# Scores of two narrow cross attentions as two 64-row groups, with half the head columns in the keys

## The reference: what is computed

```
q = x @ w_q + b_q        (4, 256, 16, 8)
k = ctx @ w_k + b_k      (4,  64, 16, 8)
v = ctx @ w_v + b_v      (4,  64, 16, 8)
scores = q . k / sqrt(8) per head; in layer 0 masked positions are replaced
x = layernorm(x + softmax(scores) @ v @ w_o + b_o)
```

## Time and profile before

| what | value |
|---|---|
| median of 3 runs | 1954.29 us (1953.05 to 1954.43) |
| the profiled execution | 1955.33 us, of which the profile's span is 1953.6 us |
| PE busy | 1400.2 us (72% of the span) |
| DVE busy | 1194.9 us (61%) |
| ACT busy | 694.5 us (36%) |
| POOL busy | 440.2 us (23%) |
| granted PE clock, mean | 0.835 of 2.4 GHz |
| `l0x`: keys block starts, attention starts, attention ends | 531.3, 537.8, 583.6 us |
| `l1x`: keys block starts, attention starts, attention ends | 899.8, 906.2, 948.8 us |

### The profile page before, as it was taken

How to read it: one execution, slowest core, us unless ns; L and a number is a source line. 1 busy time by engine, 2 the same in 40 slices (tenths; PEclk the granted TensorE clock), 3 DMA queues, 4 the chain that set the end, 5 groups by cost and what they waited for, 6 DMA issues and landing times. The chain is left out here.

```text
span 1953.6 us, 23816 instructions
## 1 busy us (share of the span) xinstructions
PE 1400.2 (72%) x8378; PEld 1055.8 (54%) x8378; DVE 1194.9 (61%) x2335; ACT 694.5 (36%) x1421; POOL 440.2 (23%) x454
## 2 busy tenths in 40 slices
PE   5888888988686985836719847587268738863785
PEld 3666666666563654714509735465237516732572
DVE  5899999999255664155595464334458277437744
ACT  3465665565132761312302220042033233423341
POOL 2566556565102002101003110000010050005000
PEclk8999899999796996967859868599679867976697
DMA  6101110110101002500014200000100000000000
GB/s 208 34 26 39 40 34 26 40 34 1 56 1 33 1 1 82 163 2 1 13 43 160 83 0 1 1 1 32 55 0 1 1 0 1 1 1 0 1 1 11
DMA packets 31030, 59.85 MB, mean 31 GB/s; under 512 B 6592, under 2 KB 17856, under 8 KB 30656
## 3 DMA queue, kind: packets, MB, share of 16 engines
q1 hardware_dynamic: 29888, 56.09, 8.9%
q0 software_dynamic: 1024, 2.23, 0.5%
HBM read 54.13 MB, written 4.18 MB: 30 GB/s over the span
## 5 line engine op out<-in xcount | busy, mean ns | idle before, releaser
L187 POOL TENSOR_TENSOR rstd<-spread,minus_half 128x4 f32<-128x4 f32 x36 | 36.8, 1023 | 960.5 <-DVE spread L169 960.5
L917 PE MATMUL l0h_scores<-l0h_k_rot,l0h_q_slots 128*128 128x128 f32 (+1 forms) x1024 | 206.9, 349 | 0.0
L917 PEld LDWEIGHTS l0h_scores<-l0h_k_rot,l0h_q_slots 128*128 128x128 f32 x1024 | 169.8, 208 | 13.2
L1134 POOL TENSOR_TENSOR l0h_k_part<-large_weights,l0h_sines 128x512 f32<-128x512 f32 x64 | 83.9, 1311 | 177.1 <-PE l0h_scores L917 129.1
L1008 ACT ACTIVATE l0h_scores<-l0h_scores,l0h_top 128x128 f32<-128x128 f32 (+1 forms) x256 | 100.4, 392 | 27.7 <-DVE l0h_top L1087 27.5
L1081 DVE TENSOR_TENSOR l0h_q_slots<-l0h_q_rot,l0h_chosen 128x1024 f32<-128x1024 f32 x64 | 78.4, 1225 | 6.7
L893 PE MATMUL l0h_projected<-XT,l0h_wq 128*128 128x256 f32 x256 | 70.1, 397 | 15.2 <-ACT large_weights L979 11.9
L1135 POOL TENSOR_TENSOR l0h_k_rot<-large_weights,l0h_cosines 128x512 f32<-128x512 f32 x64 | 80.8, 1263 | 0.0
L907 PE MATMUL l0h_scores<-l0h_key_masks,l0h_query_picks 4*128 4x128 bf16 (+1 forms) x256 | 45.0, 257 | 49.0 <-DVE l0h_probs L1104 49.0
L1087 DVE TENSOR_REDUCE l0h_top<-l0h_scores 128x2 f32<-128x256 f32 (+1 forms) x128 | 65.0, 546 | 6.6 <-PE l0h_scores L917 6.4
L1446 ACT ACTIVATE l0n_probs<-l0n_scores,l0n_top 128x256 f32<-128x256 f32 x128 | 53.8, 482 | 39.0 <-DVE l0n_top L1477 38.9
(11 more groups left out here) (718 smaller groups left out, 3658.7 us busy)
## 6 DMA issues: line engine op xcount, KB each, us to landing
l1e_experts<-in_l_experts SPq DMA_DIRECT2D x16, 768.0 KB, 4.4
l0e_experts<-in_l_experts SPq DMA_DIRECT2D x15, 578.0 KB, 4.5
l0h_chosen<-l0h_chosen_dram SPq DMA_DIRECT2D x64, 128.0 KB, 3.0
small_weights<-in_w_l_ffn SPq DMA_DIRECT2D x1, 4016.0 KB, 12.9
l0h_pos<-l0h_pos_dram SPq DMA_DIRECT2D x56, 64.0 KB, 2.0
large_weights<-in_w_l_xattn SPq DMA_DIRECT2D x1, 2632.0 KB, 9.1
l0h_wq<-in_l_wq SPq DMA_DIRECT2D x16, 128.0 KB, 2.9
large_weights<-in_w_l_attn SPq DMA_DIRECT2D x2, 512.0 KB, 4.1
```

The costliest lines, as they stand in the source:

```text
L917: mm = nc.tensor.matmul(at[:, slot], q_slots[:, s % 2, slot, part, i * P:(i + 1) * P], k_rot[:, s % 2, part, 0:KEYS[i][1]], start=False, s ...
L1134: nc.gpsimd.tensor_tensor(k_part[:], source, at_batch(sines, s), ALU.mult)
```

## The change

`keys` gets eight head columns for each batch where it had sixteen. Column j keeps head j on partitions 0 to 63 and head j + 8 on partitions 64 to 127, and is zero elsewhere. The scores of heads 0 to 7 are then a product over partitions 0 to 63 alone, into the first bank, and those of heads 8 to 15 a product over partitions 64 to 127, into the second. In layer 0 both mask products now come first, then the two score products.

```diff
-        keys = sb("keys", [P, B, HX, SC])
+        keys = sb("keys", [P, B, HX // 2, SC])
...
-                    nc.vector.tensor_tensor(keys[:, b], bc(k_t[:, b * SC:(b + 1) * SC].unsqueeze(1), [P, HX, SC]),
-                                            bc(k.own_head.unsqueeze(2), [P, HX, SC]), ALU.mult)
+                    nc.vector.tensor_tensor(keys[:, b], bc(k_t[:, b * SC:(b + 1) * SC].unsqueeze(1), [P, HX // 2, SC]),
+                                            bc(k.own_of_eight.unsqueeze(2), [P, HX // 2, SC]), ALU.mult)
...
                     if mask:
                         nc.tensor.matmul(out[:, c, :], k.ident16[:], bc(mask(t).unsqueeze(1), [P, HX // 2, SC]),
                                          start=True, stop=False, skip_group_check=True)
-                    mm = nc.tensor.matmul(out[:, c, :], q_t[:, t * P:(t + 1) * P], keys[:, b, c * 8:(c + 1) * 8, :],
-                                          start=not mask, stop=True, skip_group_check=True)
+                for c in range(2):
+                    half = slice(c * P // 2, (c + 1) * P // 2)
+                    mm = nc.tensor.matmul(out[:, c, :], q_t[half, t * P:(t + 1) * P], keys[half, b], start=not mask, stop=True,
+                                          skip_group_check=True)
```

## The result

The changed kernel takes 1946.93 us (median of 14 runs, 1942.21 to 1951.14), the kernel before 1953.22 (14 runs, 1950.52 to 1957.53). The ratio is 0.9968, 95% interval 0.9958 to 0.9978: 6.3 us faster, between 4.3 and 8.2. The time lies in the range of the prediction (1937.5 to 1949), and the sign is the forecast one, but the gain is about half of the 11.8 us of the sum.

A forecast was written before the change was run, and what follows sets the result against it. The prediction took DVE plus some POOL to bound the keys block and PE the steady attention. Keys 4.3, steady 2.7 + 2.0 and start 1.3 + 1.5 sum to 11.8 us: median 1942.5 us, range 1937.5 to 1949.

The forecast's parts named there:

- if the clock is below 1.00 between the first turn and the last score: A sign, in the profile of the attention after the change, that would show the prediction wrong; no size given.
- What bounds the stretch: Steady attention: PE sets the pace; after the change still in `l0x`, while in `l1x` ACT's copy ends last.
- Keys: Keys blocks: shorter DVE instructions, done after 2.92 us, end each block 2.13 us earlier; 4.3 us for two.
- Overlap of the two halves with 512 columns: Attention scores: 64-row passes of the two halves run two at a time, 0.43 us from pair to pair.
- no overlap: Rival on the scores: the halves do not overlap with 512 columns; about 1955 us, no change; chance 0.07.
- Price of the ways in and out: Attention units: switching to 64-row passes and back costs 0.41 us a unit; units become 4.36 and 4.03 us.
- The start: Scores at half clock before the first turn: 1.3 us saved in `l0x` and 1.5 in `l1x`, together 2.8 us.
- the clock comes up later: Rival: the clock rises later against the first turn, or later stages meet it differently; 4 us, 1946.5 us; chance 0.10.
- the clock falls: Rival in the steady stretch: half clock as PE idles; both stretches falling entirely gives 1967 us or so; chance 0.03.

The follow-up runs named there:

- masks apart: The changed kernel with each bank's mask product again right ahead of its score product; ratio 1.0039 to the kernel before, 7.6 us slower.
- sixfold one: The changed kernel with projections, keys block and attention run six times in each part, each after some 10 us of DVE-only work; median 2597.83 us.
- the keys alone: The changed kernel with eight head columns kept, but scores as full-array products over all 128 rows; ratio 0.9983 to the kernel before.
- the extra products: Unneeded PE products ahead of the first turn, in the keys block, or both, added to the changed kernel: ratios 0.9946, 0.9939, 0.9930 to the kernel before.
- products in the keys block: The changed kernel with two products of 512 float32 columns on PE while it waits for the keys; ratio 0.9939 to the kernel before.
- groups only: The kernel before, keys still with sixteen columns, but scores as two 64-row groups; ratio 0.9993 to the kernel before.

## Why the prediction was right, and by how much it was off

The terms of the sum came out nearly as worked out in the profile, except that the clock took a part of the gain back at the first turns, and the measured gain is about half of the sum. The time still lies in the range because the range was wide, 5 to 17 us, and not because this loss was counted in it. By a sign that the prediction named itself ("if the clock is below 1.00 between the first turn and the last score") its part on the clock was wrong: the clock was at 0.50 in 545.0 to 548.4 and in 906.7 to 910.2.

- **What bounds the stretch**: right. PE sets the pace in `l0x`, and in `l1x` the bound went from PE to the chain of turn, copy and W.
- **Keys**: right to 0.01 us in the profile: 2.92 us, PE's start 2.13 us earlier. POOL's instructions still end one by one beside DVE's, with four left after it. Alone it brings 3.3 us measured, 4.3 forecast, inside the interval.
- **Overlap of the two halves with 512 columns**: right, 1.13 us for four passes, and masks apart shows that adjacency is what makes it. The rival "no overlap" is out. The pairs start 0.53 us apart (551.99 and 552.52) and not 0.43, but the block as a whole takes the 1.06 us that the sum had.
- **Price of the ways in and out**: right. The units are 4.35 and 4.03 us for 4.36 and 4.03 forecast. The Trainium skill ("TensorEngine Tiling (Array Packing)", Key Properties) states that a change of the tiling mode drains TensorE. The trace agrees as far as a unit pays some 0.4 us around its 64-row passes, the price of the rows, and that does not decide.
- **The start**: DVE's first reduce comes 3.06 and 2.12 us after PE's start, 3.1 and 2.3 forecast, and the first turn follows as worked out, 1.40 and 1.68 us earlier after PE's start than before. This is the term that failed all the same: "Both lie on the chain that leads to the first turn", 1.3 + 1.5 = 2.8 us. They do, but what was won up to the first turn was lost just behind it, 1.6 and 1.5 us in the profiled execution and 2.1 us in the mean of the sixfold one. The prediction had score(1) done with "little to spare" ahead of the first turn, 3 us of work in 3.6 us, and PE had 1.7 and 2.0 us to spare. The rival "the clock comes up later" was nearest, with 0.10 and 4 us, and it saw that PE "has less to do and idles before the first turn". As it stands it names a late rise, which is two of the eight losing starts; in the other six the clock had risen and fell again at a place where no rival had it. The idle time could be read off beforehand, and deserved to be part of the main case.
- **The rival "the clock falls"**: its price is too small by its own rule. A stretch that takes 25 us at full clock lasts up to 50 at half, so that two such stretches would cost up to 50 us and not 25. Nothing in the forecast hangs on it.
- **Size**: floors without a loss give 47.46 - 41.17 + 44.21 - 38.31 = 12.2 us, the forecast being 11.8. With the mean losses of the sixfold profile, 10.0 are left; by their medians the sixfold kernels differ by 69.9 us, 11.6 for each pair of layers. Measured in the plain kernel are 6.3 (4.3 to 8.2). So 1 to 2 us are shown to go at the two starts, and some 2 to 7 remain.
- **What stays open** is where those go. They are tied to the groups (1.4 measured for 7.5 forecast) and to the clock: the mean granted clock of the timed executions falls from 0.835 to 0.8365 before to 0.832 with the groups, is 0.836 with the keys alone, and comes back to 0.834 to 0.8375 with the extra products. Taking away 12 us at full clock would lower it by 0.001; the other 0.002 to 0.0035 of 1945 us are 4 to 7 us of full clock, and the two starts of the profiled execution account for 3.2. There are two candidates, and no run decides between them. One is that the starts lose more in executions that were not profiled: single starts with more than 1.7 us lost are seen in other kernels, 2.6 us with the products in the keys block repeated sixfold, and the 20.7 us at half clock with the masks apart. The other is the rest of the network, which the change does not touch and which the prediction's rival on the clock also named: over the ten plain profiles the part ahead of `l0x` takes 530.7 to 533.6 us, the part between the stretches 318.9 to 323.5, and the part behind `l1x` 1004.9 to 1005.8 in seven and 1008.4 to 1010.4 in three (before, groups only, products in the keys block). One profile of each kernel cannot tell this scatter from an effect of the groups.

## What to carry to other kernels

Price a pair of half-array products as one, plus some 0.4 us for going in and out, and keep the pair adjacent; that is measured here at full clock with float32 products of 512 columns. When PE work is shortened ahead of a wait, look at what the clock does behind the wait: with shorter scores and a gap of 1.7 to 2.3 us, 1.5 to 1.6 us were lost in eight starts of twelve, and one useless product in the gap gave it back. The gap alone does not tell, since the kernel before had gaps of up to 1.87 us and lost nothing. Judge a 0.5% change by the timed runs and not by one pair of profiles, and repeat the stage inside one kernel to see how it scatters.

## What was not expected of the hardware

- The granted clock fell from full to half behind a gap of 1.96 us ahead of the first turn, and in a start of the same program with the same gap and the same rise of the clock it did not.
- It stayed at half for 20.7 us in which PE never stood idle by the profile, with 64-row passes one at a time between full-array ones. In the changed kernel, with the passes two at a time, it first reached full speed within 9.4 us of PE's start in each start profiled. One profile shows this, and nothing here shows that the single passes are the reason.
- A product that nothing reads made the kernel 4 us faster (10.5 for 6.3), and the sixfold one 5.4 us.
